# Attention kernel on one core: the sums of two tiles in one run, three tiles of probabilities, one copy of the rounded biases

## What is computed

```python
qkv = x.reshape(B, S, dim) @ qkv_w + qkv_b            # S = 48*48 = 2304, 12 heads of 16
attn = einsum('bqc,bkc->bqk', q * scale, k)
rel_h = einsum('bhwc,hkc->bhwk', r_q, Rh)
rel_w = einsum('bhwc,wkc->bhwk', r_q, Rw)
attn = softmax(attn + rel_h[:, :, :, :, None] + rel_w[:, :, :, None, :], axis=-1)
out = (attn @ v) ... @ proj_w + proj_b
x = x + layer(group_norm(x))                          # four layers
```

## Time and profile before

| | |
|---|---|
| median of 3 runs | 6808.59 us (6806.47 to 6817.65) |
| span of the profiled execution | 6801.4 us |
| PE busy | 6725.5 us (99%) |
| DVE busy | 5454.7 us (80%) |
| ACT busy | 4753.7 us (70%) |
| POOL busy | 938.1 us (14%) |

### The profile page before, as it was taken

The page is one execution under the profiler, slowest core; times in us unless marked ns, Lnnn a source line. Parts: engine busy times, 40 slices in busy tenths (PEclk is TensorE's granted clock), DMA queues, the critical chain, the costliest instruction groups (busy, mean ns, idle before and its releaser), DMA issues.

```text
span 6801.4 us, 139326 instructions
## 1 busy us (share of the span) xinstructions
PE 6725.5 (99%) x53600; PEld 4245.8 (62%) x53600; DVE 5454.7 (80%) x9973; ACT 4753.7 (70%) x10225; POOL 938.1 (14%) x967
## 2 busy tenths in 40 slices
PE   7999999999999999999999999999999999999998
PEld 5666666666666666666665666666666666666664
DVE  7887888778887788877888778887888878888883
ACT  3776776767767777677776767767676676767775
POOL 2111010211112110121111210102101121101110
PEclk8999999999999999999999999999999999999999
DMA  6676676767677677667676766767677676777673
GB/s 164 148 156 152 137 160 138 163 151 142 152 144 168 144 143 156 149 158 149 142 155 149 158 143 143 161 145 166 140 144 157 147 165 138 143 152 156 144 154 88
DMA packets 306307, 1013.72 MB, mean 149 GB/s; under 512 B 107440, under 2 KB 196976, under 8 KB 215920
## 3 DMA queue, kind: packets, MB, share of 16 engines
q1 hardware_dynamic: 305648, 1004.81, 68.9%
HBM read 745.26 MB, written 255.69 MB: 147 GB/s over the span
## 4 chain that ended last, share of the span: by engine, by line
PE 96%; DMA 1%; DVE 1%; issue 0%; ACT 0%; SPq 0%; POOL 0%; DVEq 0%; ACTq 0%
PE work L805 30%; PE work L878 27%; PE work L796 27%; PE work L824 7%; PE work L843 3%; PE work L862 2%; PE work L851 1%; DMA moving<-rel_scratch 1%; DVE mpart L683 1%; PE work L830 0%; DVE xb L674 0%; ACT probs L561 0%; DMA back<-attention_scratch 0%; DVE hi L721 0%; PE work L835 0%
## 5 line engine op out<-in xcount | busy, mean ns | idle before, releaser
L683 DVE TENSOR_REDUCE mpart<-work 128x1 f32<-128x512 f32 (+1 forms) x8640 | 5088.7, 632 | 1079.7 <-PE work L805 1013.1
L561 ACT ACTIVATE probs<-work 128x512 f32<-128x512 f32 (+1 forms) x8640 | 4100.2, 564 | 866.6 <-PE work L796 852.1
L805 PE MATMUL work<-mkeys,hi 128*128 128x512 f32 (+1 forms) x8640 | 3404.1, 395 | 10.6 <-DVE mpart L683 8.8
L796 PE MATMUL work<-moving,keys 113*128 113x512 f32 (+1 forms) x8640 | 3299.9, 383 | 10.9 <-DMA moving<-rel_scratch 5.7
L805 PEld LDWEIGHTS work<-mkeys,hi 128*128 128x128 f32 x8640 | 1643.6, 190 | 622.4 <-DVE mpart L683 324.0
L878 PE MATMUL work<-probs,vall 128*17 128x288 f32 x27648 | 2013.1, 409 | 0.0
L796 PEld LDWEIGHTS work<-moving,keys 113*128 113x128 f32 x8640 | 1642.1, 190 | 362.3 <-ACT probs L561 39.2
L878 PEld LDWEIGHTS work<-probs,vall 128*17 128x17 f32 x27648 | 637.3, 96 | 846.8 <-ACT probs L561 358.3
L824 PEld LDWEIGHTS work<-image,tab 128*48 128x48 f32 x6912 | 401.6, 124 | 544.9 <-ACT probs L561 513.2
L490 POOL TENSOR_TENSOR full<-full,hi 128x384 f32<-128x384 f32 x576 | 583.5, 1016 | 938.7 <-DVE hi L721 937.6
L495 POOL TENSOR_TENSOR rden<-oraw,rden 128x576 f32<-128x576 f32 x96 | 137.1, 1428 | 3955.3 <-DMA rden<-inverse_scratch 3955.3
(11 more groups left out here) (42 smaller groups left out, 646.8 us busy)
## 6 DMA issues: line engine op xcount, KB each, us to landing
moving<-rel_scratch SPq DMA_DIRECT2D x1728, 144.0 KB
moving<-qk_scratch SPq DMA_DIRECT2D x288, 576.0 KB
rel_scratch<-hi SPq DMA_DIRECT2D x192, 432.0 KB, 5.7
rel_scratch<-full SPq DMA_DIRECT2D x192, 432.0 KB, 5.5
moving<-rel_scratch SPq DMA_DIRECT2D x288, 288.0 KB
image<-qk_scratch SPq DMA_DIRECT2D x384, 144.0 KB, 3.2
keys<-qk_scratch SPq DMA_DIRECT2D x192, 288.0 KB, 7.8
qk_scratch<-split_hi SPq DMA_DIRECT2D x144, 192.0 KB, 3.9
```

What stands on the lines that cost most here:

```text
L561: act.activation(probs[:, tile % RING, lo:up], bank[:, 0:up - lo], ACT.Exp).then_inc(act_read, 1)
L683: dve.tensor_reduce(mpart[:, u % 2, q, m:m + 1], bank[:, 0:MSPLIT[m][1] - MSPLIT[m][0]], AX.X, ALU.max)\
L796: pe.matmul(bank[:, 0:up - lo], tile_of(keys[0:K_ROWS, u % 2, :], c, third), moving[0:K_ROWS, slot_of(u, third)[0], lo:up], start=True, st ...
L805: pe.matmul(bank[:, 0:up - lo], hi[:, u % 2, q * P:(q + 1) * P], mkeys[:, u % 2, lo:up], start=True, stop=True).then_inc(for_dve, 1)
```

## The change

The sums of a tile no longer follow each tile. After the scores of each even tile, the sums of the two tiles before it run in one go. For that `probs` holds three tiles (`RING`). `hi` holds one unit's rounded biases in place of two. The bias fills move from the start of tiles 0 to 11 to the end of tiles 1 to 12, and there stand ahead of the sums. The roundings move from tiles 8 to 13 to tiles 9 to 14, the stores of `hi` from tile 13 to 15 and of `full` from 14 to 16, the load of `image` from 12 to 13.

```diff
-RING = 2
+RING = 3
+REL_AT, HIGH_AT = 1, 9
...
-            if t < 12 and u + 2 < UNITS:
-                plan[u][t][0].insert(0, ("rel", u + 2, t))
+            if REL_AT <= t < REL_AT + 12 and u + 2 < UNITS:
+                plan[u][t][SB].append(("rel", u + 2, t - REL_AT))
...
-        hi = sb("hi", [P, 2, N], F32R)
+        hi = sb("hi", [P, N], F32R)
...
-                    if t == 12 and u + 3 < UNITS:
+                    if t == 13 and u + 3 < UNITS:
                         image_load(u + 3)
-                    if t == 13 and u + 2 < UNITS:
+                    if t == 15 and u + 2 < UNITS:
                         sp.wait_ge(hi_ready, NB * (u + 3))
-                        rel_store(u + 2, hi[:, (u + 2) % 2, :].bitcast(F32), 0, rel_hi_stored)
+                        rel_store(u + 2, hi[:, :].bitcast(F32), 0, rel_hi_stored)
                     if t == 14 and 0 <= u + 1 < UNITS:
                         top_load(u + 1, 0)
-                    if t == 14 and u + 2 < UNITS:
-                        sp.wait_ge(lo_ready, NB * (u + 3))
-                        rel_store(u + 2, full[:, :], 1, rel_lo_stored)
...
                         slot_load(u + 1, 2)
                         top_load(u + 1, 2)
+                    if t == 16 and u + 2 < UNITS:
+                        sp.wait_ge(lo_ready, NB * (u + 3))
+                        rel_store(u + 2, full[:, :], 1, rel_lo_stored)
...
                 if r == 0:
                     dve.wait_ge(fullq_in, 32 * (u + 1))
-                    if u >= 2:
-                        dve.wait_ge(rel_hi_stored, 32 * (u - 1))
-                dve.tensor_copy(hi[:, u % 2, cols], full[:, cols]).then_inc(hi_ready, 1)
+                    if u >= 1:
+                        dve.wait_ge(rel_hi_stored, 32 * u)
+                dve.tensor_copy(hi[:, cols], full[:, cols]).then_inc(hi_ready, 1)
...
-                        if 8 <= t < 14 and i == 2 and -2 <= u and u + 2 < UNITS:
-                            high(u + 2, t - 8)
+                        if i == 2 and HIGH_AT <= t < HIGH_AT + NB and -2 <= u and u + 2 < UNITS:
+                            high(u + 2, t - HIGH_AT)
...
                     for i in range(SB + 1):
-                        if i == SB and 0 < tile <= TILES * UNITS:
-                            attend(tile - 1)
                         for item in plan[u][t][i]:
                             fill(item)
+                        if i == SB and tile % 2 == 0 and 0 < tile <= TILES * UNITS:
+                            attend(tile - 2)
+                            attend(tile - 1)
```

More of the change, by code:

```diff
@@ L489, in low @@
                 pool.wait_ge(hi_ready, NB * u + r + 1)
-                pool.tensor_tensor(full[:, cols], full[:, cols], hi[:, u % 2, cols].bitcast(F32), ALU.subtract)\
+                pool.tensor_tensor(full[:, cols], full[:, cols], hi[:, cols].bitcast(F32), ALU.subtract)\
                     .then_inc(lo_ready, 1)
@@ L804, in fill @@
                         pe.wait_ge(mkeys_in[u % 2], 32 * (u // 2 + 1))
-                    pe.matmul(bank[:, 0:up - lo], hi[:, u % 2, q * P:(q + 1) * P], mkeys[:, u % 2, lo:up],
+                    pe.matmul(bank[:, 0:up - lo], hi[:, q * P:(q + 1) * P], mkeys[:, u % 2, lo:up],
                               start=True, stop=True).then_inc(for_dve, 1)
```

## The result

The changed kernel takes 7118.62 us (median of 4 runs), the kernel before 6810.16 us: a ratio of 1.0452, 95% interval 1.0438 to 1.0465. That is 308 us slower. The prediction had 7063 us, with a range of 6900 to 7160.

What follows compares the result with a forecast made beforehand. TensorE's instruction stream was taken as the bound. Waits of 3.67 us less 1.02 of joins give +2.65 us a unit, 254 us over 96 units: 7055 us of span, 7063 us measured; range 6900 to 7160.

Steps and rivals of the forecast that it cites:

- The mechanism: Ten L805 between two runs of sums find banks late, and fills behind scores wait for ScalarE: 3.67 us a unit.
- the walk: Item-by-item timing of a pair of tiles against VectorE's and ScalarE's banks; a pair without fills loses 0.31 us in waits.
- The added 0.05 and 0.10 of a late bank: On TensorE, a late bank costs 0.15 us beyond the end of the read: start 0.05 after it, next matmul 0.34 later.
- The sum for a plain unit: Waits of 3.67 us less 1.02 us of joins: +2.65 us a unit.
- I take every unit as a plain one: All 96 units counted at +2.65 us, 254 us in all, though units with projections have further work in some tiles.
- Joins: Changes between unlike matmuls on TensorE: 0.14 us saved a pair without fills, 0.10 with, 1.02 a unit, 98 us in all.
- twelve fills late by 0.10: Both bias fills of each of six pairs wait 0.10 us for ScalarE's bank: 1.2 us a unit.
- the score after a short fill: After a four-matmul fill the next score is due 0.07 us before its bank: three pairs, 0.2 us a unit.
- The weighed rule: Weight loads overlap matmuls in flight only where row groups differ; joins would then save nothing and the sum end at 7161.
- The other engines keep up: Rival: reads end or banks free earlier, so the waits don't come: 6711 us, chance 0.10.
- Only VectorE's waits come: Rival: fills don't wait for ScalarE, taking off 1.2 us a unit: 6948 us, chance 0.16.
- Transfers come late: Rival: the third slot's load behind the hi store misses tile 2, adding 1 to 1.5 us a unit: 7159 to 7207, chance 0.08.

Runs made afterwards that it cites:

- single_ahead: The changed kernel with the sums of one tile after every tile again, the bias fill still ahead of them: 6974.55 us, 1.0240 of the kernel before.
- single_behind: The changed kernel with the sums of one tile after every tile again and the bias fill behind them: 6819.05 us, 1.0015 of the kernel before.
- merged_ahead_both: The changed kernel with each long reduction and each long exponential over 256 columns in place of 512, for timing alone: 6734.01 us, 0.9890 of the kernel before.
- merged_ahead_halfexp: The changed kernel with each long exponential over 256 columns in place of 512, for timing alone: 6981.86 us, 1.0254 of the kernel before.

## Why the prediction was right, and where it was off

*The mechanism* held. The burst of ten L805 outruns VectorE: pair 15/16 was forecast at 6.95 us and lasts 6.99, with the same two L806 held until 2.83 and 3.43 where the walk had 2.82 and 3.42, and relief of VectorE alone takes the waits away. The fill behind the scores waits for ScalarE, most of all at the end of tile 1, where the sums copies stand ahead of the exponential:

```profile
1668.96 0.38 PE L797 MATMUL work<-moving,keys 113*128 113x256 f32 x1
1669.75 0.38 PE L825 MATMUL work<-image,tab 128*48 128x96 f32 x4 [0.41 <-ACT probs L562]
```

From start to start 0.79, where most other fills have 0.19 (one has 0.36, from 1694.40 on), so 0.60 more; the walk had 0.65 for the copies and 0.10 for the bank, 0.75. single_ahead shows the same wait without merging. The added 0.05 and 0.10 of a late bank, taken from one stretch, hold: L806 at 1723.44 is followed by L797 after 0.34.

*The sum for a plain unit* held to the second figure. I said +2.65 us. Windows over a plain unit, a unit with projections and a unit with group statistics, of the changed kernel (length, busy time and instructions of each engine, granted clock, DMA):

```profile
1661.99:1729.70 67.71, 66.71 (x544) 42.51 (x542) 52.97 (x100) 48.25 (x106) 7.46 (x7) 1.00 0.65 139
1361.37:1437.81 76.44, 74.67 (x568) 47.39 (x566) 54.46 (x100) 52.31 (x112) 16.50 (x19) 1.00 0.67 155
3838.40:3913.00 74.60, 70.67 (x548) 42.03 (x546) 64.87 (x138) 50.37 (x106) 7.45 (x7) 1.00 0.65 147
```

The same units before took 65.09, 72.70 and 69.28 us: +2.62, +3.74 and +5.32. By groups of pairs (medians of the plain units, the change less single_behind, walk in brackets): 1/2 and 13/14 together 1.28 (1.42), the five pairs between 0.96 (0.89), 15/16 and 17/0 0.36 (0.34).

*The step that failed* is "I take every unit as a plain one". It is a term of the sum that was too small. 21 units have projections of q and k and lose about 1.0 more each than the 2.65, some 21 us; 7 have group statistics and lose 2.7 to 4.7 more, 3.3 on average, some 23 us; 28 units with other extra work lose 0.3 more each, about 9 us. That is 53 of the 56 us. The experiments say why. A unit with projections loses its extra microsecond already in single_ahead, without merging (2.8 us against 1.6 of a plain unit). A unit with statistics loses by merging: 5.0 us from single_ahead to the change, where a plain unit loses 1.0, and relieving VectorE alone takes 7.4 us off it again. VectorE was near its bound there before (the earlier trace rows are of such a unit), and sorting its work into bursts costs more. A count of VectorE's and ScalarE's busy time by kind of unit was to be had from the trace.

*Joins* were undersized, and the error was hidden. L797's 256 columns to L806's 256 take 0.13 (1722.71 to 1722.84), not 0.20, and with both engines relieved the pair lasts 6.49, 0.29 below the 6.78 of two single tiles; I had 0.14. The waits took the difference back: the seventh L806, due 0.07 sooner than in the walk, is held until the same moment, and so the waits of the pair are 0.50 (6.99 less 6.49), where the walk had 0.31. The single terms inside the waits were not right either: twelve fills late by 0.10 were too many (L825 starts 0.19 after L797's 256 columns where 0.17 was assumed free, and single_ahead loses 0.1 a fill in all), while the score after a short fill lost more than 0.07. In the changed kernel's timeline, from the end of tile 3:

```profile
1676.94 0.28 PE L797 MATMUL work<-moving,keys 113*128 113x256 f32 x1
1677.13 0.38 PE L825 MATMUL work<-image,tab 128*48 128x96 f32 x4
1677.35 0.35 PE L806 MATMUL work<-mkeys,hi 128*128 128x256 f32 x1
1677.70 0.47 PE L797 MATMUL work<-moving,keys 113*128 113x512 f32 x1
```

L806 to L797 is 0.35 there, where 0.20 is undisturbed. So the sum of a plain unit is so exact partly by luck: joins too small and waits too small cancelled.

*The weighed rule* of the Trainium skill ("TensorE: Matmul & The Clock Gate", section on packing, what overlaps), that a weight load overlaps with matmuls in flight only where their row groups differ, would have let joins save nothing and ended at 7161. That is nearer to the 7118.62 than 7063 is, but not by its reason: with both engines relieved, pair 15/16 lasts 6.49 us with merged sums and 6.80 with single ones, so the joins do save.

*The rivals.* "The other engines keep up" would be the world of merged_ahead_both, which is 1.1% faster than before; its premise was false. "Only VectorE's waits come" is false by single_ahead and by merged_ahead_halfexp, where relieving ScalarE alone takes 137 us off. "Transfers come late" did not happen in the change, whose chain has 1% of DMA, but it is the next bound: with both engines relieved it is 11%.

## What to carry to other kernels

A wait for a bank was decided here by the worst burst between two pauses, not by busy shares (75% and 67% of the span): walk the items of one burst against the reader's pace, bank by bank, before taking a pause out of a stream. A long item that feeds nobody is where the readers catch up, so bundling such items costs as soon as the stretch between them outgrows the banks; and an item right behind a run of others in the same banks inherits their backlog. Bundle instead what is alike on the engine and short, as L830 with the sums.

## What was not expected of the hardware

- A matmul of 256 columns followed by one of 256 with other weights took 0.13 us from start to start, a 256-column one followed by 512 columns 0.20 to 0.23 behind sums or a fill. The cost of a join depended on what came before the pair: in merged_ahead_both the second of two 256-column matmuls was followed by 512 columns after only 0.12 us (1629.56 to 1629.68). Why, these starts don't show.
- Narrow fp32 matmuls (17 and 18 columns of weights) followed one another without most of the 0.12 us that leaving them for 128 columns costs by the prediction's estimate: 0.98 from sums to L830, 1.09 from sums to L805.
